# The end of a graph-and-experts kernel: first expert's rows summed on TensorE, plain stores with x1 added on the chip

## The chip, the cores and the metric

The kernel runs on one core of a Trainium2 chip. The metric is the time of one execution in device microseconds, and the median of several runs is compared. The profile is one execution by itself, with its own time.

## What is computed

There are 3125 rows x of 256 numbers and 53125 edges. A first layer (layer norm, neighbour means, two matrices) gives x1 = x + gnn(layernorm(x)). A second one is a mixture of 16 experts of which each row takes two. Cut to what matters at the end:

```
x1 = x + gnn(layernorm(x), ...)
h  = layernorm(x1)
for each row: the two experts with the largest gate logits, softmax weights w0, w1
y   = h + w0 * expert0(h) + w1 * expert1(h)
out = x1 + (y - mean(y)) / sqrt(var(y) + 1e-5) * gamma + beta
```

The kernel adds beta to x1 early, and it works with y multiplied by a factor for each row, (1 + ratio) * 64, where ratio = w1 / w0; the layer norm takes the factor out again through an epsilon of each row.

## The kernel before, in words

Rows stand in 25 blocks of 125 (one row per partition). The graph layer runs to about 290 us, and x1 + beta of every block is stored to `out` as it is made. Then 64 items (a tile of 128 row slots of one expert each) run through the two matrices of their expert, and GpSimd scatters each item's rows to the table `z_tab` in DRAM (`send`, L752): for each row first its first expert's result, then its second expert's. What follows from about 504 us is the end, or tail, and the change lies in it alone.

The tail goes through the 25 blocks in chunks of `TAIL` = 2, 4, 6, 6, 4, 3 blocks, and each chunk in pieces of up to two blocks (`PIECES`, 13 in all). One piece fills one PSUM bank, of which there are eight. Its steps, with the engine of each:

- **SP** loads x1 + beta back from `out` (`xb_load`, L635) into three places, long before use, and, once all items are scattered, the rows of `z_tab` chunk by chunk (L657), each chunk as two transfers: 112 partitions and 13 (`HALVES`).
- **VectorE** makes `diag` (L1744), a diagonal matrix per block that turns x1 into its layer norm; **ScalarE** makes `diag_r` (L1025), the diagonal of `ratio`.
- **TensorE** puts into the piece's bank `diag` times x1 (fp32, L1302) and gates times the experts' biases (fp16, L1303): the function `residual`. It runs six pieces ahead (`AHEAD`). When z has landed, `second_expert` adds `diag_r` times the second expert's rows (L1311). From the eighth piece on, `residual` waits until VectorE has taken the bank's earlier content (`summed`).
- **VectorE** adds the first expert's rows to the bank's content into Z (L1756), and when a chunk's pieces are all summed it takes statistics per block (L1760), aggregates them (L1765) and centres (subtract the mean, multiply by gamma, L1772), all in place in Z.
- **GpSimd** makes the rows' scales from the variances (`row_scales`, L805 to L810), six small instructions a chunk.
- **ScalarE** multiplies by the scale from Z to Y (L1032).
- **GpSimd** stores Y to `out` by DMAs that add to what is there, x1 + beta (`add_out`, L817), two per chunk. In its queue the store of chunk q - 1 stands behind the scales of chunk q.
- The last chunk is done differently: VectorE makes its scales itself (`rsqrt`, L516 to L522), then multiplies and adds x1 in one instruction per block (L1776), and SP stores it plainly (L661). SP then waits for that store (L663) and for all the adding ones (L664).

The order is written out by hand: each engine's queue is run in program order, and semaphores (`p_made`, `summed`, `moments`, `scales_made`, `centred`, `normed`, `out_ready`) join them.

```
for q in range(NT - 1):
    row_scales(q)
    if q >= 1:
        add_out(q - 1)
add_out(NT - 2)
```

Of the kernel before, what the change touches and what calls it, by code (L numbers as in the profile page):

```python
# [5 lines left out]
D = 256  # L6
# [8 lines left out]
BT = 125  # L15
# [41 lines left out]
TAIL = [2, 4, 6, 6, 4, 3]  # L57
# [16 lines left out]
def build(nc, x, src, dst, w_self, w_neigh, gnn_b, gate_w, gate_b, w1, b1, w2, b2, gamma, beta, out):  # L74
# [6 lines left out]
    with ctx:  # L81
# [226 lines left out]
        XB_MID = agg_f[:, 0:(TAIL_AT[4] - TAIL_AT[2]) * D].rearrange("p (b d) -> p b d", d=D)  # L308
        assert (TAIL_AT[4] - TAIL_AT[2]) * D <= AFTER_GT
        XB_LATE = w1_f[:, 0:(NB - TAIL_AT[4]) * D].rearrange("p (b d) -> p b d", d=D)  # L310
# [16 lines left out]
        def xb(lo, hi):  # L327
            if hi <= TAIL_AT[2]:
                return XB_EARLY[0:BT, lo:hi, :]
            if hi <= TAIL_AT[4]:  # L330
                return XB_MID[0:BT, lo - TAIL_AT[2]:hi - TAIL_AT[2], :]
            return XB_LATE[0:BT, lo - TAIL_AT[4]:hi - TAIL_AT[4], :]

# [143 lines left out]
        summed = sem("summed")  # L477
# [92 lines left out]
        def _(sp):  # L570
# [76 lines left out]
            xb_load(2)  # L647
            xb_load(3)
            sp.wait_ge(w2_copied, NITEM)
            for q in range(4, NT):  # L650
                xb_load(q)
# [6 lines left out]
            bs = slice(TAIL_AT[NT - 1], NB)  # L658
            sp.wait_ge(out_ready, 1)
            for ps in HALVES:  # L660
                sp.dma_start(out_b[ps, bs, :], Y[ps, bs, :]).then_inc(last_stored, DMA)  # L661
            sp.wait_ge(last_stored, 2 * DMA)
            sp.wait_ge(out_stored, (NT - 1) * 2 * DMA)  # L663
# [3 lines left out]
        def _(pool):  # L667
# [129 lines left out]
            def row_scales(q):  # L797

                s, n = q % 2, TAIL[q]
                y, t0, t1 = rstd3[s][:, 0:n], tmp3[0][:, 0:n], tmp3[1][:, 0:n]  # L800
                link, _ = counted_link(pool, scale_steps, 5 * q)
                pool.wait_ge(moments, q + 1)
                if q >= 2:
                    pool.wait_ge(normed, q - 1)
                link(g.tensor_tensor(t0, mv3[s][:, 0:n, 1], epsr[:, TAIL_AT[q]:TAIL_AT[q] + n], ALU.add))  # L805
                link(g.tensor_tensor(y, t0, mhalf[0:BT, 0:n], ALU.pow))
                link(g.tensor_tensor(t1, y, y, ALU.mult))
                link(g.tensor_tensor(t1, t1, t0, ALU.mult))
                link(g.tensor_scalar(t1, t1, -0.5, 1.5, ALU.mult, ALU.add))
                g.tensor_tensor(y, y, t1, ALU.mult).then_inc(scales_made, 1)  # L810

            def add_out(q):
                bs = slice(TAIL_AT[q], TAIL_AT[q + 1])
                pool.wait_ge(normed, q + 1)
                pool.wait_ge(xb_loaded[q], 2 * DMA)
                for ps in HALVES:
                    g.dma_start(out_b[ps, bs, :], Y[ps, bs, :], accum_op=ALU.add).then_inc(out_stored, DMA)  # L817

            for q in range(NT - 1):
                row_scales(q)  # L820
                if q >= 1:
                    add_out(q - 1)
            add_out(NT - 2)

        @block.scalar
        def _(act):
# [198 lines left out]
            for q in range(NT - 1):  # L1027
                act.wait_ge(scales_made, q + 1)
                act.wait_ge(centred, q + 1)
                for b in range(TAIL_AT[q], TAIL_AT[q + 1]):  # L1030
                    c = b - TAIL_AT[q]
                    ins = a.activation(Y[0:BT, b, :], Z[0:BT, b, 0, :], ACT.Copy, scale=rstd3[q % 2][:, c:c + 1])  # L1032
                ins.then_inc(normed, 1)

# [3 lines left out]
        def _(pe):  # L1038
# [251 lines left out]
            AHEAD = 6  # L1290

            def residual(i):
# [5 lines left out]
                if i >= 8:  # L1298
                    pe.wait_ge(summed, i - 7)
# [5 lines left out]
            def second_expert(i):  # L1305
# [4 lines left out]
                for b in range(lo, hi):  # L1310
                    ins = t.matmul(p_sum[i % 8][:, b - lo, :], diag_r[:, b, :], Z[0:BT, b, 1, :], start=False, stop=(b == hi - 1))  # L1311
# [12 lines left out]
        def _(dve):  # L1324
# [421 lines left out]

            i = 0
            for q in range(NT):
                s, n, b0 = q % 2, TAIL[q], TAIL_AT[q]
                z = Z[0:BT, b0:b0 + n, :, :]  # L1750
                dve.wait_ge(z_loaded[q], 2 * DMA)
                for lo, hi in PIECES:
                    if b0 <= lo < b0 + n:
                        dve.wait_ge(p_made, i + 1)
                        zs = Z[0:BT, lo:hi, 0, :]
                        v.tensor_tensor(zs, zs, p_sum[i % 8][:, 0:hi - lo, :], ALU.add).then_inc(summed, 1)  # L1756
                        i += 1
# [10 lines left out]
                if q == NT - 1:  # L1768
                    dve.wait_ge(normed, q - 1)
# [31 lines left out]
```

## Time and profile before

| what | value |
|---|---|
| runs, median of 3 | 567.57 us (565.23 to 568.28) |
| the profiled execution, its own time | 565.0 us |
| its span, first to last instruction | 563.1 us |
| mean granted TensorE clock | 0.949 |
| busy share of the span: TensorE, VectorE, ScalarE, GpSimd | 85%, 78%, 67%, 60% |
| the tail within the span, about | 504 to 563.1 us |

How to read it: the busy shares are means over the whole span, and most of it is not touched by the change. The tail is a stage of its own with limits of its own, so it is read by stretches of time. VectorE is called DVE in the rows, ScalarE ACT, GpSimd POOL, TensorE PE, and SPq is SP's queue, which issues DMAs. W and AGG are tensors in SBUF that hold many things in turn; in the tail W holds Z, Y, `diag_r` and part of x1. PS is PSUM.

### The profile page before, as it was taken

To read this page: it belongs to the slowest core of one execution; us is meant where nothing else is said; L and a number is where in the kernel's file an instruction comes from. 1 tells how busy PE (TensorE), PEld (TensorE's weight loads), DVE (VectorE), ACT (ScalarE), POOL (GpSimd) and SP (SyncE) were. 2 spreads that over 40 slices of the span, in tenths; PEclk is the share of its full clock that TensorE was granted. 3 is DMA by queue.
4 is the path that set the end of the run, shared out by engine and by line. 5 is a ranking of instruction groups with operands and counts; after the bars stand their busy time and mean duration, and the time that the engine had idled before them with its cause. 6 is when DMAs were issued, how large, how long until landed. Compare 5 with 4: busy or idle time off the path is not lost.

```text
span 563.1 us, 14414 instructions
## 1 busy us (share of the span) xinstructions
PE 479.7 (85%) x5119; PEld 410.8 (73%) x5119; DVE 439.1 (78%) x1090; ACT 379.5 (67%) x929; POOL 339.7 (60%) x479
## 2 busy tenths in 40 slices
PE   1899989999898998999934799999999999998820
PEld 0455568887787886888824698899999999896610
DVE  4888769999998999989865777676777777664794
ACT  1455656877775876866643588888888888877131
POOL 5672007777665677577410677777777777652383
PEclk9999989999998999999966799999999999999975
DMA  9410024444543344321130423632332222337989
GB/s 217 96 29 1 1 78 124 135 118 128 146 122 101 114 136 122 91 70 38 31 119 1 122 73 112 170 94 79 96 92 87 74 82 81 72 90 186 220 131 147
DMA packets 45077, 56.68 MB, mean 101 GB/s; under 512 B 5347, under 2 KB 37851, under 8 KB 45006
## 3 DMA queue, kind: packets, MB, share of 16 engines
q1 hardware_dynamic: 34736, 36.73, 24.3%
q0 software_dynamic: 9440, 18.28, 13.0%
q10 hardware_dynamic: 830, 0.74, 0.6%
q8 instruction: 42, 0.69, 0.5%
q14 instruction: 29, 0.24, 0.1%
HBM read 39.73 MB, written 17.99 MB: 102 GB/s over the span
## 4 chain that ended last, share of the span: by engine, by line
PE 49%; DVE 31%; DMA 7%; issue 5%; POOL 3%; ACT 2%; SPq 1%; DVEq 0%; ACTq 0%; POOLq 0%
PE PS L1251 13%; PE PS L1263 13%; DVE W L1405 7%; DVE W L1498 5%; PE PS L1064 4%; PE PS L1144 4%; PE PS L1145 4%; DVE oh_extra L1405 3%; PE PS L1096 3%; DMA W<-z_tab 2%; DMA arena<-xh_tab,tok_of 2%; PE PS L1239 2%; DVE AGG L1506 2%; DVE arena L1508 1%; DVE AGG L1586 1%
## 5 line engine op out<-in xcount | busy, mean ns | idle before, releaser
L1144 PE MATMUL PS<-arena,AGG 125*128 125x257 f16 x625 | 148.9, 276 | 0.0
L1145 PE MATMUL PS<-arena,AGG 125*128 125x256 f16 x625 | 148.4, 274 | 0.0
L850 ACT ACTIVATE AGG<-PS 128x500 f16<-128x500 f32 (+1 forms) x175 | 93.1, 542 | 39.6 <-PE PS L1096 36.3
L1251 PE MATMUL PS<-arena,AGG 128*128 128x128 f16 x1536 | 97.9, 221 | 1.7 <-issue 0.8
L752 POOL DMA_INDIRECT z_tab<-arena,meta_of x64 | 79.9, 1249 | 31.5 <-issue 19.5
L1263 PE MATMUL PS<-AGG,arena 128*128 128x256 f16 x768 | 95.8, 273 | 1.3 <-DVE AGG L1714 1.0
L1251 PEld LDWEIGHTS PS<-arena,AGG 128*128 128x128 f16 x1536 | 89.9, 99 | 2.9 <-DVE AGG L1708 1.6
L746 POOL DMA_INDIRECT arena<-xh_tab,tok_of x64 | 66.8, 1044 | 37.0 <-issue 17.8
L980 ACT ACTIVATE arena<-PS,arena 128x128 f32<-128x128 f32 x256 | 73.2, 369 | 10.4 <-PE PS L1251 4.0
L1263 PEld LDWEIGHTS PS<-AGG,arena 128*128 128x128 f16 x768 | 72.8, 98 | 10.1 <-DVE AGG L1714 1.2
L1405 DVE TENSOR_TENSOR W<-table,arena 128x1024 f16<-128x1024 f16 x104 | 74.7, 727 | 6.6 <-PE PS L1096 6.6
L1721 DVE TENSOR_TENSOR arena<-arena 128x512 f16<-128x512 f32 x64 | 44.3, 693 | 41.2 <-ACT arena L989 41.2
L1144 PEld LDWEIGHTS PS<-arena,AGG 125*128 125x128 f16 x625 | 61.0, 98 | 7.1
L1145 PEld LDWEIGHTS PS<-arena,AGG 125*128 125x128 f16 x625 | 61.4, 98 | 6.1
L1096 PE MATMUL PS<-W 128*128 128x125 f16 x416 | 50.5, 222 | 8.0 <-DVE W L1405 7.3
L1708 DVE COPY AGG<-W 128x2048 f16 x64 | 44.7, 698 | 15.1 <-PE PS L1251 9.7
L989 ACT ACTIVATE arena<-arena 128x512 f16<-128x512 f32 x64 | 40.3, 630 | 15.5 <-PE PS L1263 15.3
L1714 DVE COPY AGG<-W 128x2048 f16 x64 | 46.4, 725 | 0.0
L1096 PEld LDWEIGHTS PS<-W 128*128 128x128 f16 x416 | 33.7, 102 | 15.2 <-DVE W L1405 7.9
L773 POOL TENSOR_TENSOR AGG<-AGG,beta_b 125x256 f32<-125x256 f32 x25 | 21.8, 870 | 38.0 <-ACT arena L888 38.0
L972 ACT ACTIVATE arena<-PS 128x512 f16<-128x512 f16 x64 | 37.7, 590 | 10.3 <-PE PS L1239 10.2
L1498 DVE SCALAR_TENSOR_TENSOR W<-W 128x512 f16<-128x512 f32 x60 | 44.2, 737 | 0.3 <-ACT W L926 0.2
(243 smaller groups left out, 890.3 us busy)
## 6 DMA issues: line engine op xcount, KB each, us to landing
W<-in_L_ffn_w SPq DMA_DIRECT2D x60, 256.0 KB, 3.2
out<-AGG SPq DMA_DIRECT2D x25, 125.0 KB
xh_tab<-arena SPq DMA_DIRECT2D x25, 125.0 KB
W<-z_tab SPq DMA_DIRECT2D x2, 1344.0 KB
W<-z_tab SPq DMA_DIRECT2D x2, 896.0 KB
W<-in_x SPq DMA_DIRECT2D x2, 784.0 KB
AGG<-out SPq DMA_DIRECT2D x2, 672.0 KB
out<-W POOLq DMA_DIRECT2D x2, 672.0 KB, 6.9
```

What stands on the lines that cost most here:

```text
L746: g.indirect_dma_start(xsr[:, n % 4, :].bitcast(f16), None, xh_tab[:, :], bass.IndirectOffsetOnAxis(ap=tok_of[:, n:n + 1], axis=0)).then_i ...
L752: g.indirect_dma_start(z_tab[:, :], bass.IndirectOffsetOnAxis(ap=meta_of[:, n:n + 1], axis=0), yo[:, n % 4, :], None, bounds_check=2 * N - ...
L850: a.activation(AT[j % 2][:, :, QT * GD * s:QT * GD * s + n * GD].rearrange("p h (g l) -> p h g l", l=GD), (p_A0[s % 2] if j == 0 else p_A[ ...
L980: ins = a.activation(hr[:, s % 2, c * P:(c + 1) * P], p_h[s % 2][:, c * P:(c + 1) * P], ACT.Relu, bias=b1e[:, s % 2, c:c + 1], scale=1.0 / ...
L1096: t.matmul(to[:, c * BT:(c + 1) * BT], hot[:, r, :, w], hot[:, QT // PAIR + r, 0:BT, w], start=True, stop=True).then_inc(tiles_done, 1)
L1144: t.matmul(p_agg[j % 2], AT[j % 2][0:BT, h, :], HW[0:BT, h, D:HS - 1], start=(h == 0), stop=False)
L1145: ins = t.matmul(p_agg[j % 2][:, 0:D], AT[j % 2][0:BT, h, :], HW[0:BT, h, 0:D], start=False, stop=(h == NB - 1))
L1251: ins = t.matmul(p_h[s % 2][:, c * P:(c + 1) * P], w1e[:, s % 2, wa, k, c * P:(c + 1) * P], xT[:, s % 2, xa, k, :], start=(y == 0), stop=( ...
L1263: ins = t.matmul(p_y[s % 2], h[:, s % 2, c * P:(c + 1) * P], w2e[:, s, wa, c, :], start=(y == 0), stop=(y == len(terms) - 1))
L1405: v.tensor_tensor(oh[q % ORING][:, :, :, :], table[:, :, 0:PAIR].unsqueeze(1).to_broadcast([P, rows, P, PAIR]), edges[:, q, :, :].rearrang ...
L1498: v.scalar_tensor_tensor(lo, stage, scale, hi, ALU.mult, ALU.subtract).then_inc(w_lo, 1)
L1714: v.tensor_copy(w2e[:, s, :, :, :].rearrange("p a c d -> p (a c d)"), W2[:, bass.ds(e, 1), :, :, :].rearrange("p e a c d -> p (e a c d)")) ...
```

## The change

The chunks become 2, 4, 4, 4, 4, 4, 3. TensorE adds the first expert's rows as well, by a product with the identity, so that the bank holds the whole sum; VectorE takes statistics and centres straight from PSUM. `residual` runs eight pieces ahead, and later pieces wait for the centring of the chunk whose bank they take. ScalarE still multiplies by the scales for chunks 0 and 1 (`POOLED` = 2), and GpSimd then adds x1 (`add_rows`). For all later chunks VectorE multiplies and adds x1 in one instruction per block (`finish`), one chunk behind the centring. All stores are plain: SP issues both parts for the first two chunks, and afterwards SP the part of 112 partitions and ScalarE that of 13.

```diff
-TAIL = [2, 4, 6, 6, 4, 3]
+TAIL = [2, 4, 4, 4, 4, 4, 3]
+POOLED = 2
+XB_CUT = 5
...
-            for q in range(4, NT):
+            for q in range(XB_CUT, NT):
                 xb_load(q)
...
-            bs = slice(TAIL_AT[NT - 1], NB)
-            sp.wait_ge(out_ready, 1)
-            for ps in HALVES:
-                sp.dma_start(out_b[ps, bs, :], Y[ps, bs, :]).then_inc(last_stored, DMA)
-            sp.wait_ge(last_stored, 2 * DMA)
-            sp.wait_ge(out_stored, (NT - 1) * 2 * DMA)
+            for q in range(NT):
+                bs = slice(TAIL_AT[q], TAIL_AT[q + 1])
+                if q < POOLED:
+                    sp.wait_ge(added, q + 1)
+                    for ps in HALVES:
+                        sp.dma_start(out_b[ps, bs, :], Y[ps, bs, :]).then_inc(out_stored, DMA)
+                else:
+                    sp.wait_ge(finished, q - POOLED + 1)
+                    sp.dma_start(out_b[HALVES[0], bs, :], Y[HALVES[0], bs, :]).then_inc(out_stored, DMA)
+            sp.wait_ge(out_stored, NT * 2 * DMA)
...
-                if q >= 2:
+                if 2 <= q < POOLED + 2:
                     pool.wait_ge(normed, q - 1)
+                elif q >= 2:
+                    pool.wait_ge(finished, q - 1 - POOLED)
...
-            def add_out(q):
+            def add_rows(q):
+
                 bs = slice(TAIL_AT[q], TAIL_AT[q + 1])
                 pool.wait_ge(normed, q + 1)
                 pool.wait_ge(xb_loaded[q], 2 * DMA)
-                for ps in HALVES:
-                    g.dma_start(out_b[ps, bs, :], Y[ps, bs, :], accum_op=ALU.add).then_inc(out_stored, DMA)
+                g.tensor_tensor(Y[0:BT, bs, :], Y[0:BT, bs, :], xb(bs.start, bs.stop), ALU.add).then_inc(added, 1)

             for q in range(NT - 1):
                 row_scales(q)
-                if q >= 1:
-                    add_out(q - 1)
-            add_out(NT - 2)
+                if 1 <= q <= POOLED:
+                    add_rows(q - 1)
...
-            for q in range(NT - 1):
+            for q in range(POOLED):
                 act.wait_ge(scales_made, q + 1)
...
+            for q in range(POOLED, NT):
+                bs = slice(TAIL_AT[q], TAIL_AT[q + 1])
+                act.wait_ge(finished, q - POOLED + 1)
+                act.dma_start(out_b[HALVES[1], bs, :], Y[HALVES[1], bs, :]).then_inc(out_stored, DMA)
...
-            AHEAD = 6
+            AHEAD = 8
...
                 if i >= 8:
-                    pe.wait_ge(summed, i - 7)
+                    pe.wait_ge(centred, CHUNK_OF[i - 8] + 1)
...
-            def second_expert(i):
+            def expert_sums(i):
...
                 for b in range(lo, hi):
+                    t.matmul(p_sum[i % 8][:, b - lo, :], ident[0:BT, 0:BT], Z[0:BT, b, 0, :], start=False, stop=False)
                     ins = t.matmul(p_sum[i % 8][:, b - lo, :], diag_r[:, b, :], Z[0:BT, b, 1, :], start=False, stop=(b == hi - 1))
...
-            for i in range(len(PIECES)):
-                second_expert(i)
-                if i + AHEAD < len(PIECES):
-                    residual(i + AHEAD)
+            ahead = AHEAD
+            for q in range(NT):
+                for i in range(len(PIECES)):
+                    if CHUNK_OF[i] == q:
+                        expert_sums(i)
+                while q >= 1 and ahead < len(PIECES) and CHUNK_OF[ahead - 8] <= q - 1:
+                    residual(ahead)
+                    ahead += 1
...
+            def finish(q):
+
+                n, b0 = TAIL[q], TAIL_AT[q]
+                if q < NT - 1:
+                    dve.wait_ge(scales_made, q + 1)
+                dve.wait_ge(centred, q + 1)
+                dve.wait_ge(xb_loaded[q], 2 * DMA)
+                for c in range(n):
+                    ins = v.scalar_tensor_tensor(Y[0:BT, b0 + c, :], Z[0:BT, b0 + c, 0, :], rstd3[q % 2][:, c:c + 1], xb(b0, b0 + n)[:, c, :], ALU.mult, ALU.add)
+                ins.then_inc(finished, 1)
...
-                z = Z[0:BT, b0:b0 + n, :, :]
-                dve.wait_ge(z_loaded[q], 2 * DMA)
+                sums = []
                 for lo, hi in PIECES:
                     if b0 <= lo < b0 + n:
                         dve.wait_ge(p_made, i + 1)
-                        zs = Z[0:BT, lo:hi, 0, :]
-                        v.tensor_tensor(zs, zs, p_sum[i % 8][:, 0:hi - lo, :], ALU.add).then_inc(summed, 1)
+                        for b in range(lo, hi):
+                            sums.append(p_sum[i % 8][:, b - lo, :])
+                            ins = v.bn_stats(stats3[0:BT, b - b0, :], sums[-1])
                         i += 1
-                dve.wait_ge(summed, i)
-                for c in range(n):
-                    ins = v.bn_stats(stats3[0:BT, c, :], z[:, c, 0, :])
...
                 for c in range(n):
-                    ins = v.scalar_tensor_tensor(z[:, c, 0, :], z[:, c, 0, :], mv3[s][:, c, 0:1], gamma_b, ALU.subtract, ALU.mult)
+                    ins = v.scalar_tensor_tensor(Z[0:BT, b0 + c, 0, :], sums[c], mv3[s][:, c, 0:1], gamma_b, ALU.subtract, ALU.mult)
                 ins.then_inc(centred, 1)
-            dve.wait_ge(centred, NT)
-            for c in range(n):
-                ins = v.scalar_tensor_tensor(Y[0:BT, b0 + c, :], z[:, c, 0, :], rstd3[s][:, c:c + 1], xb(b0, NB)[:, c, :], ALU.mult, ALU.add)
-            ins.then_inc(out_ready, 1)
+                if q - 1 >= POOLED:
+                    finish(q - 1)
+            finish(NT - 1)
```

## Rows read from the trace of the kernel before

**Rows 1.** Stretches: length, busy us (instructions) of PE, PEld, DVE, ACT, POOL, clock, DMA share, GB/s.
```profile
512.00:540.00 28.00, 21.75 (x97) 16.50 (x95) 18.18 (x51) 9.68 (x28) 11.69 (x22) 0.94 1.06 230
...
552.50:556.50 4.00, 0.00 (x0) 0.00 (x0) 2.71 (x7) 0.00 (x0) 1.80 (x2) 0.50 1.18 170
559.00:561.50 2.50, 0.00 (x0) 0.00 (x0) 0.00 (x0) 0.00 (x0) 0.00 (x0) 0.50 0.84 207
...
518.50:522.00 3.50, 3.35 (x9) 2.60 (x10) 0.69 (x1) 0.91 (x2) 1.06 (x5) 0.54 1.07 291
```

**Rows 2.** The chain that ended last, in order of time: start, us, what.
```profile
511.82 13.39 DMA W<-z_tab
...
530.39 0.70 DVE W L1756
```

**Rows 3.** TensorE in order of time: start, us, engine, line, instructions merged, idle before.
```profile
507.65 0.67 PE L1302 MATMUL PS<-arena,AGG 125*125 125x256 f32 x2 [0.36 <-DVE AGG L1744]
...
518.65 1.90 PE L1311 MATMUL PS<-W 125*125 125x256 f32 x4 [2.15 <-DMA W<-z_tab]
...
522.36 1.03 PE L1311 MATMUL PS<-W 125*125 125x256 f32 x4
523.22 0.59 PE L1302 MATMUL PS<-AGG 125*125 125x256 f32 x2
523.76 0.59 PE L1302 MATMUL PS<-AGG 125*125 125x256 f32 x2
525.35 1.10 PE L1311 MATMUL PS<-W 125*125 125x256 f32 x4 [0.88 <-DMA W<-z_tab]
...
540.39 1.53 PE L1311 MATMUL PS<-W 125*125 125x256 f32 x6 [1.62 <-DMA W<-z_tab]
```

**Rows 4.** VectorE in order of time, chunk 3 and the last one.
```profile
536.13 1.88 DVE L1756 TENSOR_TENSOR W<-W,PS 125x512 f32<-125x512 f32 x3
538.05 2.06 DVE L1760 BATCH_NORM_STATS2 arena<-W 125x6 f32<-125x256 f32 x6
540.14 0.51 DVE L1765 BATCH_NORM_AGGREGATE arena<-arena 125x2 f32<-125x6 f32 x6
540.68 2.46 DVE L1772 SCALAR_TENSOR_TENSOR W<-W,arena 125x256 f32<-125x256 f32 x6
...
550.33 0.16 DVE L516 TENSOR_TENSOR arena<-arena,epsr 125x3 f32<-125x3 f32 x1
...
554.03 1.28 DVE L1776 SCALAR_TENSOR_TENSOR W<-W,arena 125x256 f32<-125x256 f32 x3
```

**Rows 5.** GpSimd and SP in order of time: a chunk's scales, the last stores.
```profile
526.04 0.20 POOL L805 TENSOR_TENSOR arena<-arena,epsr 125x4 f32<-125x4 f32 x1 [6.14 <-DVE arena L1765]
...
528.41 0.20 POOL L810 TENSOR_TENSOR arena<-arena 125x4 f32<-125x4 f32 x1
...
549.84 4.47 POOL L817 DMA_DIRECT2D out<-W  x4 [0.32 <-issue]
555.34 2.01 SPq L661 DMA_DIRECT2D out<-W  x2
```

**Rows 6.** Waits of SP's queue: who waited for whom, total us, times, longest us.
```profile
SPq L663 <- DMA out<-W: 4.1, 1, 4.1
SPq L81 <- DMA out<-W: 0.9, 1, 0.9
```

**Rows 7.** Groups of instructions over the whole span: count, busy us, mean ns, idle before.
```profile
L773 POOL TENSOR_TENSOR AGG<-AGG,beta_b 125x256 f32<-125x256 f32 x25 | 21.8, 870 | 38.0 <-ACT arena L888 38.0
...
L1506 DVE SCALAR_TENSOR_TENSOR AGG<-PS,arena,AGG 125x256 f32<-125x256 f32 x25 | 12.1, 485 | 0.9
...
L1772 DVE SCALAR_TENSOR_TENSOR W<-W,arena 125x256 f32<-125x256 f32 x25 | 10.5, 480 | 0.2
```

**Rows 8.** DMA issues over the whole span: KB each, median us to landing.
```profile
W<-in_L_ffn_w SPq DMA_DIRECT2D x60, 256.0 KB, 3.2
...
AGG<-in_L_ffn_w SPq DMA_DIRECT2D x1, 512.0 KB, 4.8
```

More of the change, by code:

```diff
@@ L307, in build @@
         assert AFTER_GT + WPLACE + D <= (KC + 1) * AGGW
-        XB_MID = agg_f[:, 0:(TAIL_AT[4] - TAIL_AT[2]) * D].rearrange("p (b d) -> p b d", d=D)
-        assert (TAIL_AT[4] - TAIL_AT[2]) * D <= AFTER_GT
-        XB_LATE = w1_f[:, 0:(NB - TAIL_AT[4]) * D].rearrange("p (b d) -> p b d", d=D)
+        XB_MID = agg_f[:, 0:(TAIL_AT[XB_CUT] - TAIL_AT[2]) * D].rearrange("p (b d) -> p b d", d=D)
+        assert (TAIL_AT[XB_CUT] - TAIL_AT[2]) * D <= AFTER_GT
+        XB_LATE = w1_f[:, 0:(NB - TAIL_AT[XB_CUT]) * D].rearrange("p (b d) -> p b d", d=D)
         Y = w1_f[:, NB * D:2 * NB * D].rearrange("p (b d) -> p b d", d=D)
@@ L329, in xb @@
                 return XB_EARLY[0:BT, lo:hi, :]
-            if hi <= TAIL_AT[4]:
+            if hi <= TAIL_AT[XB_CUT]:
                 return XB_MID[0:BT, lo - TAIL_AT[2]:hi - TAIL_AT[2], :]
-            return XB_LATE[0:BT, lo - TAIL_AT[4]:hi - TAIL_AT[4], :]
+            return XB_LATE[0:BT, lo - TAIL_AT[XB_CUT]:hi - TAIL_AT[XB_CUT], :]
         PS = ctx.enter_context(nc.psum_tensor("PS", [P, 8, 512], f32))
@@ L476, in build @@
         p_made = sem("p_made")
-        summed = sem("summed")
         moments = sem("moments")
@@ L482, in build @@
         normed = sem("normed")
-        out_ready = sem("out_ready")
+        added = sem("added")
+        finished = sem("finished")
         out_stored = sem("out_stored")
-        last_stored = sem("last_stored")
         out_b = out.rearrange("(b p) d -> p b d", p=BT)
@@ L646, in _ @@
             sp.wait_ge(gates_made, 1)
-            xb_load(2)
-            xb_load(3)
+            for q in range(2, XB_CUT):
+                xb_load(q)
             sp.wait_ge(w2_copied, NITEM)
-            for q in range(4, NT):
+            for q in range(XB_CUT, NT):
                 xb_load(q)
@@ L1768, in _ @@
                 if q == NT - 1:
-                    dve.wait_ge(normed, q - 1)
+                    dve.wait_ge(finished, q - 1 - POOLED)
                     rsqrt(v, link, mv3[s][:, 0:n, 1], [last_tmp[:, w * n:(w + 1) * n] for w in range(2)], rstd3[s][:, 0:n], epsr[:, b0:b0 + n])
                 for c in range(n):
-                    ins = v.scalar_tensor_tensor(z[:, c, 0, :], z[:, c, 0, :], mv3[s][:, c, 0:1], gamma_b, ALU.subtract, ALU.mult)
+                    ins = v.scalar_tensor_tensor(Z[0:BT, b0 + c, 0, :], sums[c], mv3[s][:, c, 0:1], gamma_b, ALU.subtract, ALU.mult)
                 ins.then_inc(centred, 1)
-            dve.wait_ge(centred, NT)
-            for c in range(n):
-                ins = v.scalar_tensor_tensor(Y[0:BT, b0 + c, :], z[:, c, 0, :], rstd3[s][:, c:c + 1], xb(b0, NB)[:, c, :], ALU.mult, ALU.add)
-            ins.then_inc(out_ready, 1)
+                if q - 1 >= POOLED:
+                    finish(q - 1)
+            finish(NT - 1)
 _INS = ["x", "src", "dst", "L0_gnn_W_self", "L0_gnn_W_neigh", "L0_gnn_b", "L0_ffn_gate_w", "L0_ffn_gate_b",
```

## The prediction, made before the changed kernel was run

> **What bounds the kernel now.** I began with the 4 us table by stage, because the change touches only the end. From 512 to 540 us the DMA engines are full (share 1.06, 230 GB/s) while VectorE works 18 of 28 us and TensorE 22 [rows 1]: the stage waits for the loads of z. The chain of waits agrees up to 525 (13.4 us of z loads); then come TensorE's matmuls, and from 530.39 it is VectorE's alone to its last instruction [rows 2]. Where a chunk's z lands shows in TensorE's waits: 518.65 (6 blocks there), 525.35 (12 blocks), 540.39 (all 25) [rows 3]; that is 1.12 us per block, then 15.04/13 = 1.16. The third view is VectorE's order of time in the chunk of six [rows 4]: sums 1.88/3 per pair, so 0.31 a block, statistics 0.35, aggregation 0.09, centring 0.41, each right behind the last. So the last 25 us of computing are VectorE's own. The last view is what follows its end at 555.31 (554.03 + 1.28): SP issues the last store for 2.0 us [rows 5], waits 4.1 for it and 0.9 more for the accumulating stores [rows 6], which leaves 0.7 to the end of the span. Until 559 the engines still move accumulating stores, at 170 GB/s with a share of 1.18, and afterwards the plain one at 207, its fading end included [rows 1]. So the kernel ends 7.8 us after VectorE: GpSimd issued the stores of chunks 3 and 4 together only at 549.84, 4.47 us long [rows 5].
>
> **The change, part by part.** *Sums.* Twelve pair additions and a single one go from VectorE: 25 x 0.31 = 7.8 us. TensorE gets a second fp32 matmul per block. A pair costs 0.86 us at the full clock (522.36 to 523.22) and a residual block 0.54 (523.22 to 523.76) [rows 3]; so a block of expert sums becomes 0.87.
>
> *Eight residual pieces ahead, not six.* They are 16 blocks: 507.65 + 16 x 0.54 = 516.3 [rows 3]. Chunk 0 is then summed by 518.2, later than now, a loss that the wait for chunk 1 (518.65) covers. Then TensorE has no gap: chunk 1 four blocks 3.5 us, residual 1.1, chunk 2 3.5, residuals 2.2, chunk 3 3.5, together 13.8. Chunk 3's sums stand at 532.5. Its z, four blocks per chunk at 1.12, is there by 527.7 and chunk 2's by 523.2, so here TensorE is the bound and not the loads. The residuals now wait for the centring of an earlier chunk, which holds its PSUM piece longer; behind such a wait stand the next chunk's sums. Centring of chunks 0, 1, 2 ends at 520.2, 525.1, 529.7, before TensorE reaches the waits (522.3, 526.9, 532.5), so this costs nothing; without that cover the delay goes straight into 532.5.
>
> *VectorE reads PSUM.* Statistics and centring take the sums from PSUM. The trace has no statistics from PSUM; for the three-operand form it has both, 485 ns from PSUM and 480 from SBUF [rows 7]. I take no extra, as the nearest rows say. Upper bound +0.07: the whole 485 ns instead of the pace of 0.41, as if neighbours no longer overlapped. Lower bound -0.10 for a centring: half a pair's sum from PSUM, 0.31, is the cheapest read of 256 elements here [rows 4].
> The Trainium skill (VectorE: DVE Perf Modes, the section on the TRN2 errata) gives PSUM sources 62 more cycles per instruction than SBUF ones, 0.065 us at 0.96 GHz; the pair of rows disagrees with it, and by it the sum below would end 1.8 us later (28 instructions).
>
> *The last step of a chunk.* For chunks 2 to 5 it moves from ScalarE and an accumulating store to VectorE: row scale and x1 in one instruction, 1.28 us for three [rows 4], 1.7 for four. Those are 16 blocks more, 6.7 us. Against 7.8 saved VectorE gains 1.1, and a seventh chunk costs some 0.1.
>
> *VectorE's new end.* From 532.5, when chunk 3's second pair is there: 0.7 + 0.4 + 1.65 and chunk 2's finish 1.7 make 537.0. Chunks 4 and 5 are 1.4 + 0.4 + 1.65 + 1.7 = 5.15 each: 547.3. The last chunk: statistics 1.05, aggregation 0.3, its own reciprocal root 2.4 (550.33 to 554.03 less three centrings) [rows 4], centring 1.25, finishing chunk 5 1.7 and itself 1.3, 8.0 together: 555.3. So **VectorE ends where it did**. Z for chunks 4 to 6 (532.2, 536.8, 540.4) is early enough. Each finish waits for its chunk's scales, and the next chunk's statistics stand behind it.
>
> *Scales and the adds on GpSimd.* A chunk's scales take 2.6 us (526.04 to 528.61) [rows 5]. The x1 adds of chunks 0 and 1 are 0.87 us a block [rows 7], 1.7 and 3.5 us, in place of issuing stores; queued behind them is only the next row scale, whose new waits (an earlier chunk finished) are met long before. Chunk 1's add runs about 530.7 to 534.2, so chunk 3's scales come at 536.8, and VectorE wants them at 540.5. Hidden with 3.7 us to spare.
>
> *Stores.* The accumulating ones go; SP issues nine plain ones behind its z loads (14 of them now, not 12), each waiting for its chunk with only later stores behind it; ScalarE issues the 13-partition parts from chunk 2 on, five, with nothing behind them. Up to chunk 4 they lie beside VectorE's work: 540 to 553 has room for 18 blocks of 128 KB. What counts is the pair at the end: chunk 5 is finished at 554.0, chunk 6 at 555.3. Issue to landing was 3.2 us for 256 KB and 4.8 for 512 KB [rows 8]. 336 KB alone would be 3.7 us: 559.0. Behind chunk 5's 448 KB (4.4 us: 558.4) at 207 GB/s it is 560.0. These are loads; for plain stores the trace has only the crowded one. I take 559.5, plus 0.7 from landing to the end: **560.2**.
>
> **Sum.** 563.1 - 560.2 = 2.9 us off the span. The profiled execution took 565.0, 1.9 more than its span; the runs' median is 567.57, 2.6 above it. From the median: 567.57 - 2.9 = 564.7. Half a percent, 2.8 us, is what a measurement of this kernel can tell from no change, so the forecast lies barely beyond it.
>
> **Rivals.**
> *PSUM reads are dear.* From 532.5 on 13 statistics and 15 centrings read PSUM. At 0.07 us each, the upper bound, VectorE ends 2.0 us later: gain 0.9, **566.7**. For: nothing here has measured statistics from PSUM. Against: 485 against 480 ns [rows 7]. Chance 0.20.
>
> *The tail keeps its length.* If plain stores take as long to land as the crowded ones did, the end stays 7.8 us behind VectorE: **567.6**. For: no plain store alone is timed. Against: 207 against 170 GB/s [rows 1], and no longer the ten blocks of chunks 3 and 4 ahead of the last store. Chance 0.11.
>
> *GpSimd holds VectorE.* Should chunk 1's add overlap chunk 2's finish, VectorE loses at most the add, 3.5 us: **568.2**. It decides once the add slips by 1.3 us or more. Chance 0.05.
> The Trainium skill (SBUF — State Buffer, Reading the diagram in SBUF: two separate sides) says that a VectorE instruction with two SBUF inputs and a GpSimd one that reads SBUF exclude each other for a whole instruction; it is this mechanism, and no row here shows it for so long an add.
>
> *TensorE's clock falls, and TensorE becomes the bound*: the slower side. After a wait of 2.15 us TensorE ran from 518.5 to 522 at a mean of 0.54, which is mostly 1.2 GHz: 1.90 us for a pair that took 1.03 at 2.4 GHz [rows 1, 3]. The place is 518.65 to 532.5, where the 13.8 us of matmuls now set VectorE's start. Each microsecond at the lower level delays the end by half of one: above 5.8 us the gain is gone, above 11.4 the kernel is slower by half a percent, and at the lower level throughout it loses 13.8 and comes to 567.6 + 10.9 = **578.5**. Against: the wait before 518.65 shrinks to some 0.4 us, and after one of 0.88 the matmuls at 525.35 were quick (1.10) [rows 3]. Chance 0.08.
>
> **How the numbers follow.** The forecast has 0.56. Its own range is a gain of 2.4 to 4.9: landing between 559.0 and 560.0, and 1.5 us more if 15 centrings from PSUM cost 0.10 less. 0.45 of the 0.56 I put beyond half a percent, since the open price can only add there, and 0.11 within. With the first three rivals' 0.36, of which 0.02 (the add, with a late store) falls out on the slower side, that is faster 0.45, same 0.45, slower 0.10. The range goes from 562.4 (a gain of 5.2) to 568.0, which takes in the dear PSUM and the unchanged tail and leaves out the clock.
>
> **What would show it.** Right: a pair's four passes 0.86 at the clock 1.0 and twice as many; chunk 3's sums by 532 to 533; no VectorE wait from there on; its last instruction at 555 to 556; SP's last wait under 4 us, no accumulating store. Statistics well above 0.35 each would be the first rival; SP waiting over 6 us after VectorE the second; a finish of chunk 2 beside a GpSimd add the third; granted clock near 0.5 between 519 and 532 the fourth. The forecast is wrong if VectorE's end moves by more than 1 us either way, or if the end is not bound by VectorE and one store.

## The result, and the profile after

| | before | after |
|---|---|---|
| runs of the first pair, median | 566.53 us (4 runs, 565.23 to 568.28) | 560.67 us (4 runs, 558.76 to 562.62) |
| ratio, 95% interval | | 0.9879 [0.9836, 0.9922] |
| the profiled execution, its own time and span | 565.0 and 563.1 us | 558.76 and 556.7 us |
| start of the tail (TensorE's first transposition of gates) | 505.76 us | 503.39 us |
| length of the tail, to the end of the span | 57.34 us | 53.32 us |
| in the tail: VectorE's last instruction ends at | 49.55 us | 49.24 us |
| from there to the end | 7.79 us | 4.09 us |

The kernel is faster by 5.9 us, where 2.9 were forecast: the right side, but 560.67 us lies outside the range (562.4 to 568.0). The spans differ by 6.4 us, of which 2.4 arise ahead of the tail, where the two kernels run the same work, and 4.0 in it.

In the stretches of the changed kernel (columns as in [rows 1]) TensorE is now busy for 27.63 of 28 us, and at 520 us, where the kernel before had a clock of 0.54, it is granted 1.00. After VectorE's end, at 552.62, plain stores alone move, at 244 GB/s against 170 and then 207 [rows 1]. In 3.5 us that is some 850 KB, far more than the last chunk's 375: the store of chunk 5 moves together with it, and both have moved by 556.

```profile
512.00:540.00 28.00, 27.63 (x135) 23.23 (x134) 19.33 (x63) 4.81 (x14) 14.14 (x32) 1.00 1.00 239
...
520.00:523.50 3.50, 3.50 (x19) 2.97 (x18) 3.35 (x12) 0.19 (x1) 1.82 (x5) 1.00 1.09 235
...
552.50:556.00 3.50, 0.00 (x0) 0.00 (x0) 0.12 (x1) 0.00 (x0) 0.00 (x0) 0.50 0.85 244
...
553.50:554.00 0.50, 0.00 (x0) 0.00 (x0) 0.00 (x0) 0.00 (x0) 0.00 (x0) 0.50 0.94 303
...
555.50:556.00 0.50, 0.00 (x0) 0.00 (x0) 0.00 (x0) 0.00 (x0) 0.00 (x0) 0.50 0.27 92
```

TensorE in order of time, the changed kernel. The 16 residual blocks are done and chunk 0's sums begin at 514.09. The wait for chunk 1's z is 0.37 us, against 2.15 [rows 3], because two more residual pieces and twice the passes of chunk 0 fill that time. One product of a block (two matmul records) takes 0.43 us from start to start, so the two products of a block take 0.86, which is what a pair of blocks took before.

```profile
514.09 0.60 PE L1321 MATMUL PS<-W,ident 125*125 125x256 f32 x2
...
516.35 0.67 PE L1321 MATMUL PS<-W,ident 125*125 125x256 f32 x2 [0.37 <-DMA W<-z_tab]
516.85 0.59 PE L1322 MATMUL PS<-W 125*125 125x256 f32 x2
```

The chain that ended last, in order of time. Where it was z loads up to 525 and VectorE from 530.39 [rows 2], it is z loads up to 516.2, TensorE from there to chunk 3's sums (530.24) and VectorE to 552.62.

```profile
508.54 7.67 DMA W<-z_tab
...
529.36 0.43 PE PS L1321 x2
529.79 0.45 PE PS L1322 x2
530.61 0.43 DVE arena L1782
...
550.64 1.98 DVE W L1770 x5
```

VectorE in order of time: statistics and centring now come from PSUM, and the finish of a chunk follows the next one's centring.

```profile
530.26 0.76 DVE L1782 BATCH_NORM_STATS2 arena<-PS 125x6 f32<-125x256 f32 x2 [0.96 <-PE PS L1322]
531.05 0.38 DVE L1788 BATCH_NORM_AGGREGATE arena<-arena 125x2 f32<-125x6 f32 x4
531.47 1.66 DVE L1795 SCALAR_TENSOR_TENSOR W<-PS,arena 125x256 f32<-125x256 f32 x4
533.05 1.66 DVE L1770 SCALAR_TENSOR_TENSOR W<-W,arena,AGG 125x256 f32<-125x256 f32 x4
...
539.72 1.42 DVE L1782 BATCH_NORM_STATS2 arena<-PS 125x6 f32<-125x256 f32 x4
...
549.77 2.85 DVE L1770 SCALAR_TENSOR_TENSOR W<-W,arena 125x256 f32<-125x256 f32 x7
```

From 530.26 on VectorE waits for no other engine. GpSimd's x1 adds (0.64 and 0.59 us a block) end at 524.98 and 530.59, ahead of the next scales:

```profile
523.71 1.27 POOL L824 TENSOR_TENSOR W<-W,arena 125x512 f32<-125x512 f32 x1
...
528.24 2.35 POOL L824 TENSOR_TENSOR W<-W,arena 125x1024 f32<-125x1024 f32 x1
531.51 0.20 POOL L812 TENSOR_TENSOR arena<-arena,epsr 125x4 f32<-125x4 f32 x1 [0.92 <-DVE arena L1788]
```

SP's last issues, and the wait of its queue behind them (us in total, times, longest). The last issue ends at 552.97 and the wait of 3.4 us at 556.4: the last store has landed 3.7 us behind VectorE's end, and 0.3 are left to the end of the span. The kernel before waited 4.1 and 0.9 and had 0.7 left [rows 6].

```profile
551.47 1.50 SPq L667 DMA_DIRECT2D out<-W  x2
```

```profile
SPq L83 <- DMA out<-W: 3.4, 1, 3.4
```

### The profile page after: what moved, and what is told of

It reads as the page before. It is cut to its first block, busy times and chain, and to the rows that moved or that the text cites. A ratio compares the mean times of both kernels' runs of the same rounds, so it can differ in the third digit from the quotient of the medians.

```text
span 556.7 us, 14509 instructions
## 1 busy us (share of the span) xinstructions
PE 485.5 (87%) x5169; PEld 418.5 (75%) x5169; DVE 437.6 (79%) x1093; ACT 372.5 (67%) x913; POOL 331.1 (59%) x477
## 4 chain that ended last, share of the span: by engine, by line
PE 53%; DVE 33%; DMA 5%; issue 4%; ACT 2%; POOL 1%; DVEq 0%; ACTq 0%; SPq 0%; POOLq 0%
PE PS L1261 13%; PE PS L1273 13%; DVE W L1420 8%; PE PS L1074 6%; DVE W L1513 5%; PE PS L1154 4%; PE PS L1155 4%; DVE oh_extra L1420 4%; PE PS L1106 3%; DMA arena<-xh_tab,tok_of 2%; PE PS L1249 2%; DVE AGG L1521 2%; DVE arena L1523 2%; DMA W<-z_tab 1%; PE PS L1063 1%
## 5 line engine op out<-in xcount | busy, mean ns | idle before, releaser
L1154 PE MATMUL PS<-arena,AGG 125*128 125x257 f16 x625 | 147.3, 274 | 0.0
L1155 PE MATMUL PS<-arena,AGG 125*128 125x256 f16 x625 | 146.8, 273 | 0.0
```

The source lines that it names most:

```text
L1154: t.matmul(p_agg[j % 2], AT[j % 2][0:BT, h, :], HW[0:BT, h, D:HS - 1], start=(h == 0), stop=False)
L1155: ins = t.matmul(p_agg[j % 2][:, 0:D], AT[j % 2][0:BT, h, :], HW[0:BT, h, 0:D], start=False, stop=(h == NB - 1))
```

## The experiments

Two things had to be explained: why the tail gained 4.0 us and not 2.9, and where 2.4 us ahead of it come from. The theory was that the first lies in the last stores and the second is scatter from execution to execution. The rivals were that the change also acts ahead of the tail, and that the gain in the tail is TensorE's clock. "Tail" is the length from the first transposition of gates to the end of the span, in the profiled execution. Ratios are to the kernel before, on the same chip.

### Both kernels again, four times each

No edit.

> The kernel before, unchanged. In the two profiles the end stage (from the first gate transpose, L1285, to the end of the span) took 57.3 us before and 53.3 after, so 4.0 of the 6.4 us between the spans lie in it; the other 2.4 arose before it, where nothing is edited: 1.6 of them at 75 us, where TensorE's clock was granted at half for 3.4 us in the one execution and not in the other. Theory A, the 2.4 are chance of the execution: the stage begins elsewhere than 505.8 here (503 to 507), its length is 57.3 within 0.5, and the ratio to the kernel before is 1.000 within 0.003. Theory B, the edits move the clock's low stretches in every execution: the stage begins at 505.8 within 0.3 again.

> The changed kernel, unchanged. Theory A: the stage's length is 53.3 again within 0.5, its beginning lies elsewhere than at 503.4, and the ratio is near 0.993 (4.0 of 566). Theory B: the beginning is at 503.4 within 0.3 again and the ratio stays at 0.988 to 0.989 (6.4 of 566).

> The kernel before, unchanged, for a third look at its stage and its beginning. If the 4 us of the stage are the change's and the rest is chance: the stage 57 to 58.5 us, its beginning within 503 to 507, the ratio 1.000 within 0.004. If the two first looks at the changed kernel were lucky in the stage, this one has 54 to 56.

> The changed kernel, unchanged, for a third look: the stage 53.3 to 53.9 us, VectorE's end at 49.2 to 49.9 and 4.0 to 4.1 us from there to the end, the beginning within 503 to 507, the ratio 0.990 to 0.993 if the stage is all that the change gains.

> The kernel before, unchanged, one more execution. Theory A (the whole gain lies in the tail, and the three looks at either kernel are typical): the tail starts anywhere between 503 and 507 us and lasts 57.1 to 58.3 us. Theory B (the change also gains ahead of the tail): the kernel before starts its tail 1.5 us or more later than the changed one in the mean of all looks. Theory C (the tail of the kernel before is often longer than three looks showed, by a longer stretch of the lower granted clock): the tail lasts 59 us or more here or in the next look, with 6.8 us or more of low clock in it.

> The changed kernel, unchanged, one more execution. Theory A: its tail starts between 503 and 507 us and lasts 53.3 to 53.9 us. Theory B: it starts 1.5 us or more earlier than the kernel before in the mean of all looks, so at 503 or below. Theory C: 53.3 to 53.9 us as in A, with no low clock in the tail while TensorE has work.

> The kernel before, unchanged, one more execution, expectations as for the fourth look at it: A a tail of 57.1 to 58.3 us, B a start later than the changed kernel's by 1.5 us or more in the mean, C a tail of 59 us or more with 6.8 us or more of low clock in it.

> The changed kernel, unchanged, one more execution, expectations as for the fourth look at it: A and C a tail of 53.3 to 53.9 us and a start between 503 and 507, B a start at 503 or below.

Kernel before against itself: 1.0007 [0.9975, 1.0040] and 1.0012 [0.9985, 1.0039]. Changed kernel: 0.9906 [0.9873, 0.9940] (561.58 against 567.79 us) and 0.9906 [0.9872, 0.9941] (560.45 against 565.74). The fourth and fifth are single runs: 565.52 and 568.31 us before, 563.63 and 559.59 after, and 571.73 for one more run of the kernel before beside them. With the first pair there are five profiled executions of each; all in us:

| profiled execution | lower clock near 75 us | tail starts | TensorE's wait for chunk 1's z | lower clock before TensorE is done | VectorE's end in the tail | from there | tail |
|---|---|---|---|---|---|---|---|
| before, 1st | yes | 505.76 | 2.15 | 3.4 | 49.55 | 7.79 | 57.34 |
| 2nd | yes | 505.96 | 2.91 | 6.8 | 50.96 | 7.29 | 58.25 |
| 3rd | no | 503.12 | 2.53 | 3.4 | 50.09 | 7.03 | 57.12 |
| 4th | yes | 506.52 | 2.23 | none | 49.30 | 7.69 | 56.99 |
| 5th | yes | 506.42 | 4.02 | 6.8 | 51.99 | 7.84 | 59.83 |
| after, 1st | no | 503.39 | 0.37 | none | 49.24 | 4.09 | 53.32 |
| 2nd | yes | 505.60 | 0.96 | none | 49.81 | 4.03 | 53.84 |
| 3rd | no | 504.32 | 0.71 | none | 49.55 | 4.04 | 53.59 |
| 4th | yes | 504.73 | 2.29 | 3.4 | 52.82 | 4.03 | 56.86 |
| 5th | no | 504.42 | 0.22 | none | 49.07 | 4.04 | 53.12 |

The means of the tail are 57.91 and 54.15: 3.76 us, of which 0.28 come before VectorE's end (50.38 and 50.10) and 3.48 after it (7.53 and 4.05). The means of the start differ by 1.07 us, and the start goes with a lower clock near 75 us. Two executions of the same kernel show that this is scatter: TensorE stood for 2.18 us in both, and only in one did the clock fall. The first execution of the kernel before, TensorE in order of time:

```profile
73.62 0.34 PE L1096 MATMUL PS<-oh_extra 128*128 128x125 f16 x3 [2.18 <-issue]
...
75.25 0.42 PE L1145 MATMUL PS<-arena,AGG 125*128 125x256 f16 x1
```

The third execution of the kernel before, the same view:

```profile
73.73 0.33 PE L1096 MATMUL PS<-oh_extra 128*128 128x125 f16 x3 [2.18 <-issue]
...
75.28 0.27 PE L1145 MATMUL PS<-arena,AGG 125*128 125x256 f16 x1
```

Over all kernels below, those with the old code up to the tail start it at 505.6 in the mean (6 executions) and those with the new at 505.2 (12 executions, 503.4 to 507.0). The lower clock near 75 us came in five of the 6 and in eight of the 12. So nothing shows that the change acts ahead of the tail; a difference of 0.4 us is well within the scatter.

Not every expectation came true. The second execution of the kernel before started within 0.3 us of the first, as the rival would have it, and its tail was longer than expected; the third start (503.12) spoke against the rival. The fourth of the changed kernel missed its range of 53.3 to 53.9 by 3 us, and the fifth of the kernel before, with 59.83, is the long tail at the lower clock that theory C named.

The table also tells of the clock. In four of five the kernel before ran part of its tail at 1.2 GHz. That is little of the gain: its fourth execution had none of it and took 56.99, 3.5 more than the mean of the four such ones of the changed kernel (53.47), so of the 3.76 some 0.2 are the clock's. This rests on that one execution. The changed one fell to 1.2 GHz once, when it waited 2.29 us for z. TensorE of its fourth execution in order of time:

```profile
519.61 0.67 PE L1321 MATMUL PS<-W,ident 125*125 125x256 f32 x2 [2.29 <-DMA W<-z_tab]
...
521.75 1.06 PE L1322 MATMUL PS<-W 125*125 125x256 f32 x2
...
523.96 0.59 PE L1321 MATMUL PS<-W,ident 125*125 125x256 f32 x2
```

and its clock in that stretch (columns as above):

```profile
520.00:523.50 3.50, 3.50 (x11) 2.70 (x10) 0.65 (x2) 0.91 (x2) 0.42 (x3) 0.52 1.07 219
```

That is 3.4 us more than the mean of its other four: here the late z and the clock go straight into the end, where the same 3.4 us at the lower clock cost the kernel before 0.1 to 0.4 (57.12 and 57.34 against 56.99); 6.8 us of it went with 1.3 and 2.8 more (58.25 and 59.83). A wait of this size does not always bring the clock down: in the fourth execution of the kernel before TensorE was quick after 2.23 us (1.10 where [rows 3] had 1.90).

```profile
519.38 1.10 PE L1311 MATMUL PS<-W 125*125 125x256 f32 x4 [2.23 <-DMA W<-z_tab]
```

### Sums on TensorE, but the stores of before

```diff
-POOLED = 2
+POOLED = 6
...
-                g.tensor_tensor(Y[0:BT, bs, :], Y[0:BT, bs, :], xb(bs.start, bs.stop), ALU.add).then_inc(added, 1)
+                for ps in HALVES:
+                    g.dma_start(out_b[ps, bs, :], Y[ps, bs, :], accum_op=ALU.add).then_inc(out_stored, DMA)
...
```

> TensorE's sums, the new chunks and VectorE's reads from PSUM, but scales by ScalarE and accumulating stores by GpSimd as before for all chunks but the last. VectorE loses 16 finishing steps of 0.40, 6.4 us, though the last sums (z at 37 us into the stage) hold it: its end at 44 to 45 us into the stage instead of 49.2. If the stores are what is left, their 2.8 MB at 170 GB/s and a last issue near 43 us with 7 to 10 us to landing end the stage at 51 to 53 us, ratio 0.99. If the plain stores are the gain, as my forecast had it, the stage is 56 us or more, ratio 0.998 or above.

ScalarE scales all chunks but the last and GpSimd stores them by accumulating. Ratio 0.9913 [0.9882, 0.9944], tail 54.52: 1.05 more than the changed kernel's 53.47, and between the two cases expected (51 to 53, and 56 or more). VectorE ends at 44.48 in the tail, 5 us earlier, and the stores take all of it back. GpSimd in order of time, then SP's waits:

```profile
545.39 4.32 POOL L823 DMA_DIRECT2D out<-W  x4 [0.33 <-issue]
```

```profile
SPq L666 <- DMA out<-W: 8.0, 1, 8.0
```

GpSimd issues the last four for 4.32 us and SP then waits 8.0, while the engines move 178 GB/s:

```profile
549.00:553.00 4.00, 0.00 (x0) 0.00 (x0) 0.10 (x1) 0.00 (x0) 0.71 (x1) 0.50 1.17 178
```

So with the accumulating stores the end is theirs, and a VectorE that is done sooner is worth nothing beyond them.

### The new stores, but VectorE's pair additions

```diff
-                    t.matmul(p_sum[i % 8][:, b - lo, :], ident[0:BT, 0:BT], Z[0:BT, b, 0, :], start=False, stop=False)
...
-                        for b in range(lo, hi):
-                            sums.append(p_sum[i % 8][:, b - lo, :])
-                            ins = v.bn_stats(stats3[0:BT, b - b0, :], sums[-1])
+                        zs = Z[0:BT, lo:hi, 0, :]
+                        v.tensor_tensor(zs, zs, p_sum[i % 8][:, 0:hi - lo, :], ALU.add).then_inc(summed, 1)
...
-                    ins = v.scalar_tensor_tensor(Z[0:BT, b0 + c, 0, :], sums[c], mv3[s][:, c, 0:1], gamma_b, ALU.subtract, ALU.mult)
+                    ins = v.scalar_tensor_tensor(z[:, c, 0, :], z[:, c, 0, :], mv3[s][:, c, 0:1], gamma_b, ALU.subtract, ALU.mult)
```

> The changed kernel with the pair additions back on VectorE (25 x 0.31 = 7.8 us more of VectorE, one fp32 product per block less on TensorE). If VectorE bounds the stage from its first third on, the stage is 4 to 6 us longer than with the change, 57 to 59 us, and the ratio is 1.00 within 0.005: finishing on VectorE and plain stores without TensorE's sums give nothing. If TensorE's second product had cost as much as it saved, the stage stays at 53 to 54 us.

Ratio 0.9936 [0.9910, 0.9961], tail 56.01, less than the 57 to 59 expected. VectorE ends at 51.98, 2.6 later than in the changed kernel (49.42 in the mean of the four executions at the full clock), and the end follows 4.04 behind it, as there. From chunk 1's sums on VectorE has no gap, where in the changed kernel it waits for TensorE up to 530.26; so it ends 2.6 us later and not by all of the 7.8 us of pair additions. In order of time:

```profile
543.11 1.27 DVE L1781 TENSOR_TENSOR W<-W,PS 125x512 f32<-125x512 f32 x2
544.42 1.41 DVE L1785 BATCH_NORM_STATS2 arena<-W 125x6 f32<-125x256 f32 x4
...
546.27 1.70 DVE L1797 SCALAR_TENSOR_TENSOR W<-W,arena 125x256 f32<-125x256 f32 x4
547.90 1.66 DVE L1770 SCALAR_TENSOR_TENSOR W<-W,arena,AGG 125x256 f32<-125x256 f32 x4
```

This kernel has the same instructions with SBUF as their source: 1.41 and 1.70 us for four, where the changed one has 1.42 and 1.66 from PSUM.

### The old chunks

```diff
-TAIL = [2, 4, 4, 4, 4, 4, 3]
+TAIL = [2, 4, 6, 6, 4, 3]
...
-XB_CUT = 5
+XB_CUT = 4
```

> The changed kernel with the old chunks 2, 4, 6, 6, 4, 3. By my working the chunk size carries nothing: about 0.1 us per chunk of VectorE, so 53 to 54.5 us for the stage and the ratio of the change within 0.003. If the smaller chunks are a part of the gain (earlier statistics, no long wait for a chunk of six), the stage is 55 us or more.

Ratio 1.0014 [0.9974, 1.0055], tail 56.07, where 53 to 54.5 were expected if the chunk size carries nothing. In the medians nothing of the gain is left (567.99 against 567.31 us). The profiled execution, one of the shorter of its ten (564.99; 563.76 to 570.89), has a tail 1.8 us shorter than the mean of the kernel before and 2.6 longer than 53.47. Its mean granted clock is 0.963, that of the five runs above 569 us 0.951 to 0.955: a clock that falls in most runs of this version is a rival to the chunk size itself, and no trace here settles it. TensorE waits 1.76 us for the z of the first chunk of six. VectorE in order of time: it waits three times for TensorE within chunk 2, and can centre only when all six sums are there.

```profile
527.84 0.76 DVE L1782 BATCH_NORM_STATS2 arena<-PS 125x6 f32<-125x256 f32 x2 [1.94 <-PE PS L1322]
529.57 0.76 DVE L1782 BATCH_NORM_STATS2 arena<-PS 125x6 f32<-125x256 f32 x2 [0.96 <-PE PS L1322]
531.29 0.76 DVE L1782 BATCH_NORM_STATS2 arena<-PS 125x6 f32<-125x256 f32 x2 [0.97 <-PE PS L1322]
...
532.64 2.44 DVE L1795 SCALAR_TENSOR_TENSOR W<-PS,arena 125x256 f32<-125x256 f32 x6
```

The larger the chunk, the longer VectorE stands with only statistics to do; centring six (2.44) and finishing six are then left for after the sums.

### Six pieces ahead, and seven in the kernel before

```diff
-            AHEAD = 8
+            AHEAD = 6
...
-                while q >= 1 and ahead < len(PIECES) and CHUNK_OF[ahead - 8] <= q - 1:
+                while q >= 1 and ahead < len(PIECES) and CHUNK_OF[max(ahead - 8, 0)] <= q - 1:
```

> The changed kernel with six residual pieces ahead instead of eight, so that TensorE waits some 3 us for chunk 1's z and does two more residual pieces (2.2 us) between the expert sums. If TensorE is the bound up to chunk 3's sums, the stage is 2.2 us longer, 55.7 us; if its clock also falls in that wait (3.4 us at half), 57 to 57.5 us. If TensorE has room there, it stays at 53.5.

Ratio 0.9958 [0.9920, 0.9997], tail 57.51, 4.0 more, as expected for both effects together. TensorE waits 2.64 us for z, runs at half the clock, and does the two pieces (2.2 us) afterwards, on the path. Its order of time and its clock:

```profile
519.92 0.67 PE L1321 MATMUL PS<-W,ident 125*125 125x256 f32 x2 [2.64 <-DMA W<-z_tab]
...
521.19 1.06 PE L1321 MATMUL PS<-W,ident 125*125 125x256 f32 x2
```

```profile
520.50:524.00 3.50, 3.50 (x10) 2.75 (x9) 0.76 (x2) 0.91 (x2) 0.05 (x1) 0.51 1.08 214
```

In the kernel before:

```diff
-            AHEAD = 6
+            AHEAD = 7
```

> The kernel before with seven residual pieces ahead instead of six, so that TensorE's wait for chunk 1's z shrinks by 1.1 us and its clock may not fall there. If the low stretch at 519 us was part of what the change gained in the stage, the stage is 55 to 56.5 us instead of 57.3 and 58.3, ratio 0.997; if the z loads and VectorE set the stage anyway, it stays at 57.3 or above.

Ratio 1.0052 [1.0007, 1.0096], tail 59.73: no gain there, and the clock fell all the same. TensorE in order of time:

```profile
519.87 1.10 PE L1311 MATMUL PS<-W 125*125 125x256 f32 x4 [2.50 <-DMA W<-z_tab]
...
522.50 1.91 PE L1311 MATMUL PS<-W 125*125 125x256 f32 x4
```

A single piece more does not cover the wait there, which is still 2.50 us; it is covered in the changed kernel, where chunk 0 also has twice the passes.

### GpSimd adds x1 for more chunks

The first edit lets ScalarE and GpSimd finish all chunks but the last:

```diff
-POOLED = 2
+POOLED = 6
...
+            if POOLED == NT - 1:
+                add_rows(NT - 2)
...
```

> The changed kernel with POOLED = 6: ScalarE scales and GpSimd adds x1 for all chunks but the last, stores still plain. With the sums alone (accumulating stores) VectorE ended 44.5 us into the stage but the stores 10 us later; with plain stores the end came 4.05 us after VectorE. If both hold together, GpSimd's chain (scales 2.6, adds 2.35 per chunk of four) ends chunk 5 at about 45.3 us, and the stage is 49 to 50 us instead of 53.5: ratio 0.983. If VectorE's finishing was needed because GpSimd cannot keep up or holds VectorE, the stage stays at 53 us or more.

Ratio 0.9878 [0.9816, 0.9940], tail 52.29, where 49 to 50 were expected. VectorE was freed of 16 blocks of finish (6.3 us), yet ends only 0.5 us sooner (48.92 against 49.42). VectorE in order of time, in its own reciprocal root:

```profile
547.32 2.34 DVE L521 SCALAR_TENSOR_TENSOR arena<-arena 125x3 f32<-125x3 f32 x1
549.70 2.26 DVE L522 TENSOR_TENSOR arena<-arena 125x3 f32<-125x3 f32 x1
551.99 0.16 DVE L523 SCALAR_TENSOR_TENSOR arena<-arena 125x3 f32<-125x3 f32 x1
```

and GpSimd at the same time:

```profile
547.30 2.34 POOL L824 TENSOR_TENSOR W<-W,AGG 125x1024 f32<-125x1024 f32 x1
549.60 2.33 POOL L824 TENSOR_TENSOR W<-W 125x1024 f32<-125x1024 f32 x1
```

Two instructions of three columns, 0.16 us each elsewhere, last as long as the add beside them: 4.3 us. The rest of the 6.3 went mostly into waits for TensorE: within chunk 4, which had none in the changed kernel, 0.49 and 0.96 us. Then the same with four chunks, so that no add runs so late:

```diff
-POOLED = 2
+POOLED = 4
```

> The changed kernel with POOLED = 4. With GpSimd adding for all chunks but the last, two of the reciprocal root's instructions on three columns took 2.34 and 2.26 us instead of 0.16, each beside one of GpSimd's adds of 1024 columns. If it is those adds that held VectorE, then with no add left after chunk 3's (done 38 us into the stage, before the last chunk's root) all twelve take 0.16 to 0.2 again, VectorE ends at 47.7 us and the stage is 51.7 us, against 53.6 with the change and 52.3 with all adds on GpSimd; ratio about 0.987. If the long instructions had another cause, they stay.

Ratio 0.9884 [0.9858, 0.9909], tail 52.12; VectorE ends at 47.75, and every instruction of the root takes 0.16 or 0.17 again. And with five, chunk 4's add ahead of chunk 5's scales:

```diff
-POOLED = 2
+POOLED = 5
...
+                if q == NT - 2:
+                    add_rows(q - 1)
                 row_scales(q)
-                if 1 <= q <= POOLED:
+                if 1 <= q < NT - 2:
                     add_rows(q - 1)
...
```

> POOLED = 5, with chunk 4's add moved ahead of chunk 5's scales in GpSimd's queue, so that it runs at about 38 to 40.3 us. By the exclusion of adds and two-input instructions it meets the root's beginning by about 0.6 us only; VectorE saves one more finish of 1.6: its end at 46.8, the stage 50.9 us, ratio about 0.986. If the root meets the whole add, VectorE loses 2 us and the stage is 52 to 53 us.

Ratio 0.9873 [0.9840, 0.9906] (557.95 us, the changed kernel 560.45 on the same chip), tail 50.33, VectorE's end at 46.20. Only one small instruction still meets the add, for 0.61 us. VectorE, then GpSimd:

```profile
543.86 0.61 DVE L517 TENSOR_TENSOR arena<-arena,epsr 125x3 f32<-125x3 f32 x1
...
547.89 2.85 DVE L1772 SCALAR_TENSOR_TENSOR W<-W,arena 125x256 f32<-125x256 f32 x7
```

```profile
539.78 4.67 POOL L824 TENSOR_TENSOR W<-W,AGG 125x1024 f32<-125x1024 f32 x2
```

This version has the shortest tail of all: 3.1 us shorter than the changed kernel's 53.47, one execution against four. By the medians it is ahead of the changed kernel by 2.5 us, but the two intervals overlap.

## Why the prediction was right in its way and wrong in its size

Less 2.37 us, by which the changed kernel's tail began earlier, the prediction's moments can be held against the rows.

- *Sums, and eight pieces ahead*: right. The first expert sum was due at 513.9 and came at 514.09, chunk 3's sums at 530.1 and came at 530.24. TensorE had no gap but 0.37 us. Centring of chunks 0 to 2 was due to end at 517.8, 522.7, 527.3, and ended at 517.97, 522.95, 527.49, so no residual waited.
- *VectorE reads PSUM, no extra*: right; the first rival falls. Four statistics take 1.42 from PSUM and 1.41 from SBUF, four centrings 1.66 and 1.70. The Trainium skill (VectorE: DVE Perf Modes, TRN2 errata) has 62 cycles more for a PSUM source, an estimate of 0.26 us for four; these rows disagree with it.
- *VectorE ends where it did*: right within 0.3 (due at 552.9, ended at 552.62; 0.28 earlier in the mean of five executions). The last chunk and chunk 5's finish are one gapless run, as summed.
- *Scales and adds on GpSimd*: hidden, as forecast; an add costs 0.59 us a block, not 0.87. Chunk 3's scales are there at 534.37 (due 534.4), but by luck: the add was done 1.2 us early, the scales then waited 0.92 for VectorE's aggregation and took 2.9 us instead of 2.6. The third rival did not occur, as the add met only reads of PSUM.
- *Stores*: **this is the term that failed.** "I take 559.5, plus 0.7 from landing to the end" is 4.2 and 0.7, 4.9 us behind VectorE's end. The store landed 3.7 behind it and 0.3 were left: 4.09, and 4.03 to 4.04 in the other executions. I put the landing between "alone" (3.7, from loads) and "behind chunk 5 at 207 GB/s" (4.7). It was as early as alone, but it was not alone: the stores of chunks 5 and 6 moved together, and did so at 244 GB/s, up to 303, where the sum had 207. The 0.7 was read where SP had last waited for accumulating stores; behind the plain one it is 0.3. Together that is 0.8 us of the missing gain, and VectorE's 0.3 the rest of the tail in the first pair.
- *The sum*: put right by this 0.8, it gives 563.9, still inside the range, so the store alone does not explain why the median fell below it. Of the 4.0 us between 564.7 and 560.67, 0.8 are the store and 0.3 VectorE's end. Another 1.0 is the starting value, a median of three (567.57) that a fourth run took to 566.53. For the other 1.9 us no step is shown to have failed. In the profiled pair 2.37 us arose ahead of the tail, and there the changed kernel's start was early by chance (503.39 against a mean of 504.49). One early start does not move a median, though, and the repeats gained 6.2 and 5.3 us; in the means of five the tail gains 3.76 and the start 1.07. The cause of this part stays open.
- *The clock in the tail of the kernel before* was left out. I saw its 3.5 us at 0.54 and asked only whether the change would bring more of it. It was there in four executions of five before and in one of five after, and is worth some 0.2 us in the means.
- *TensorE's clock falls*, the rival with 0.08, is real as an event: one execution in five, at the place that was named, with 3.4 us and not 13.8. It did not turn the sign.
- "*A seventh chunk costs some 0.1*" named the price of a smaller cut and not its worth. It was in the sums by way of chunk 3's time, but I never asked what the same change does with chunks of six: a tail 2.6 us longer, and nothing gained in the medians.

What stays open: the medians differ by 5.3 to 6.2 us, the five profiled executions by 4.8 (3.76 and 1.07). With spans between 560.2 and 566.3 for one kernel and 556.7 and 561.6 for the other, five executions cannot decide whether the last microsecond is more than scatter. Nor is the share of each part settled: every version with one part taken away has a single profiled execution, and for the old chunks it and the medians do not agree.

## What to carry to other kernels

When the path runs from one engine to the next, take the end apart into the last engine's end and what follows it, and price both by rows that resemble the new ending; here VectorE's end came within 0.3 us and the store behind it was off by 0.8. A forecast from one execution inherits its chance: compare starts of the changed stage before crediting a difference to the change, and profile more than one. Parts of a change need each other (stores, sums, chunk size, pieces ahead): taking one away at a time shows that none carries the gain by itself. Without it the tail is longer by 1.1 us (stores), 2.5 (sums), 2.6 (chunks of four) and 4.0 (eight pieces ahead), where the whole change gains 3.8.

## What the runs showed of the hardware that had not been expected

A long GpSimd add of two SBUF tensors holds VectorE instructions with two SBUF inputs until it ends, however small they are: three columns took 2.34 and 2.26 us instead of 0.16, beside adds of 2.34 and 2.33. Instructions with one SBUF input, or with PSUM as one of two, were not held: beside the add of 542.60 to 544.97 in the same kernel (GpSimd adds for all chunks but the last) the aggregation took its 0.38 and four centrings their 1.66. GpSimd, then VectorE:

```profile
542.60 2.37 POOL L824 TENSOR_TENSOR W<-W,AGG 125x1024 f32<-125x1024 f32 x1
```

```profile
543.24 0.38 DVE L1790 BATCH_NORM_AGGREGATE arena<-arena 125x2 f32<-125x6 f32 x4
543.65 1.66 DVE L1800 SCALAR_TENSOR_TENSOR W<-PS,arena 125x256 f32<-125x256 f32 x4
```

The Trainium skill (SBUF — State Buffer, Reading the diagram in SBUF: two separate sides) states this exclusion; the trace agrees, and adds that the size of the VectorE instruction does not matter.

The same wait does not give the same clock: after 2.18 us near 74 us, and after 2.15 to 2.3 in the tail, TensorE was granted 2.4 GHz in some executions and 1.2 in others of the same kernel.
